# Attention values in one stationary tile: high and low parts side by side, their products added afterwards, and output blocks that hold both heads

## The chip, the cores and the metric

The kernel runs on one core of a Trainium2 chip. A core has TensorE (PE; its weight loads are shown as a queue of their own, PEld), VectorE (DVE), ScalarE (ACT), GpSimd (POOL) and SyncE (SP), which starts the transfers. Each works through its own instructions in order, and they wait for one another through semaphores. The metric is the time of one execution on the device in microseconds (us); lower is better.

## What is computed

The reference is a layer of two parts over 8 sequences of 512 rows and 256 columns. The first is a Mamba block (convolution, selective scan). The second, in which the change lies, is attention with mixtures of experts for values and outputs, then a feed-forward block. Cut to the part that matters:

```
D, H, P, E, K, F = (256, 16, 64, 8, 2, 1024)
def _moe_attn(x, Wq, Wk, Wv, Wo, Wsel_v, Wsel_o):
    q = _rope(jnp.einsum('bsd,hdp->bhsp', x, Wq))
    k = _rope(jnp.einsum('bsd,hdp->bhsp', x, Wk))
    gv = _gate(x, Wsel_v)
    v = jnp.einsum('bsd,bhse,hedp->bhsp', x, gv, Wv)
    att = jax.nn.softmax(jnp.einsum('bhsp,bhtp->bhst', q, k) / np.sqrt(P), axis=-1)
    o = jnp.einsum('bhst,bhtp->bhsp', att, v)
    go = _gate(x, Wsel_o)
    return jnp.einsum('bhsp,bhse,hepd->bsd', o, go, Wo)
```

There are 16 heads of 64 columns. `_gate` keeps the two largest of 8 expert scores in each row. An output of a head is multiplied by the gates of its 8 experts, which gives 8 x 64 rows for the contraction with `Wo`.

## The kernel before

The program has three stages. `stage_a` is the Mamba block, `stage_c` the feed-forward block. `stage_b` is the attention: the outer loop runs over 8 pairs of heads, the inner one over the 8 sequences, so there are 64 **batches** (one pair of heads, one sequence), with the same instructions in each. The last batch of a pair (`more_pairs`) also prepares the weights of the next pair; 7 of the 64 do so, and I call the end of such a batch a pair boundary.

Products are made of two parts: a float32 operand is split into a high part (a copy rounded by the type) and a low part (the operand minus the high part), and high*high, high*low and low*high are added in PSUM. ACT makes the high parts, DVE or POOL the low ones. `product` issues the three matmuls.

In a batch, TensorE runs in this order (function `batch` under `block.tensor`): `values` (expert values) mixed with `scores`; 16 transposes of 128x128 for the first head's probabilities (`turn_probabilities`); `attend(it, 0, c)` for 4 chunks c of the rows; 16 transposes for the second head and 4 of the gates (`turn_gates`); `attend(it, 1, c)`; then `spread_gates` 0 to 3 (they spread the output gates over the partitions, two blocks each) among the two `project_raw` (query and key of the next batch); then `project(it, j, n)` for 8 output blocks n.

`attend` multiplies the values, held still in the array, by the turned probabilities. The values of a head have 64 columns. Before, they lie twice side by side in each of two tiles (`vv[0]` high, `vv[1]` low, 128 columns each), so the output has the head's 64 rows twice, and one block of 128 rows is one head with two experts: blocks 0 to 3 are of the first head and need only `oT[:, 0]`, blocks 4 to 7 of the second. ACT copies these outputs out of PSUM (`keep_outputs`), DVE multiplies two blocks at a time by the spread gates (`gate_outputs` p = 0 to 3), ACT takes the high part (`high_outputs`), and the low part is POOL's for blocks 0 to 3 and DVE's for blocks 4 to 7 (`low_outputs`). `project(n)` waits for the low part of block n.

What else matters on the other engines: DVE does the rope of the next batch (`turn_raw`: two multiplications and a shuffle in place; `rotate`: their sum, into `qk_full`, which before shares its memory with `oT`), then `low_qk`; `tops` and POOL's `rank_one` to `rank_four` alternate to find the two largest gates of the next batch, ending in `gates`, which the next `gate_values` needs; `low_half` on POOL makes the low parts of `wv` and `wo` for the next pair. DVE's order in the tail is set by the order of calls in its `batch`:

```
                gate_outputs(it, 2)
                gate_outputs(it, 3)
                if more or more_pairs:
                    turn_raw(it + 1)
                    rotate(it + 1)
                low_outputs(it, 0)
                low_outputs(it, 1)
                if more or more_pairs:
                    tops(*coming, 2)
                low_outputs(it, 2)
                low_outputs(it, 3)
```

## Time and profile before

| what | value |
|---|---|
| three runs | 4522.73, 4522.21 and 4515.9 us, median 4522.21 |
| the profiled execution | 4524.23 us in all, its span 4522.4 us |
| PE (matmuls) | busy 3882.3 us, 86% of the span |
| PEld (weight loads) | busy 2704.3 us, 60% |
| DVE | busy 3556.1 us, 79% |
| POOL | busy 2873.1 us, 64% |
| ACT | busy 2045.4 us, 45% |
| granted TensorE clock | 0.911 of full speed over the span, 0.99 to 1.00 in the attention |

Stage B takes from about 1476 us (the first low part of `wv`) to about 4200 us of the span. Busy time of PE says little by itself: the records of successive matmuls overlap (each lasts 0.39 us while they start 0.23 us apart), so what PE's work costs is read from the starts, and what it waits for from the idle time in brackets.

### The profile page before, as it was taken

What the parts mean: (1) busy time and instruction counts of PE and PEld (TensorE: products, weight loads), DVE (VectorE), ACT (ScalarE), POOL (GpSimd) and SP (SyncE); (2) the same over time, 40 slices, a digit from 0 to 9 for tenths busy, and PEclk for the clock granted to TensorE, in tenths of its full rate; (3) what the DMA queues carried; (4) which work ended last, traced back from release to release, by engine and by line L of the source; (5) the groups of instructions that cost most, each with busy time, mean ns of one, the idle gap of its engine ahead of it and who ended that gap; (6) DMA issues with size and microseconds to landing.
All of it is one profiled execution on the core that took longest, in us unless ns stands there. A gap on an engine that the chain in (4) does not pass through costs nothing. (4 is left out here: it accounts for less than half of the span.)

```text
span 4522.4 us, 54798 instructions
## 1 busy us (share of the span) xinstructions
PE 3882.3 (86%) x16256; PEld 2704.3 (60%) x16256; DVE 3556.1 (79%) x3884; ACT 2045.4 (45%) x3761; POOL 2873.1 (64%) x2524
## 2 busy tenths in 40 slices
PE   6777776777764899999999999999999999999887
PEld 2233333333322677777777777777777777777676
DVE  5999999999995677677777677677677677677598
ACT  4544544545532344444444444444444444444443
POOL 2757757758663666666666766766666666666444
PEclk8887777877876999999999999999999999999898
DMA  1000000000002100000000000000100100000001
GB/s 37 0 10 14 24 9 14 24 10 14 19 10 95 45 14 14 35 14 14 35 10 18 35 9 19 35 9 9 39 14 9 39 14 9 19 14 12 31 28 42
DMA packets 48727, 97.83 MB, mean 22 GB/s; under 512 B 3571, under 2 KB 33139, under 8 KB 46229
## 3 DMA queue, kind: packets, MB, share of 16 engines
q1 hardware_dynamic: 47620, 92.94, 5.9%
q0 software_dynamic: 1040, 4.19, 0.2%
q8 instruction: 19, 0.31, 0.0%
q14 instruction: 48, 0.39, 0.0%
HBM read 80.34 MB, written 16.78 MB: 21 GB/s over the span
## 5 line engine op out<-in xcount | busy, mean ns | idle before, releaser
L702 DVE TENSOR_TENSOR_SCAN state<-dA,dBx 128x2048 f32<-128x2048 f32 x128 | 726.5, 5676 | 26.3 <-POOL y_part L289 21.3
L1230 ACT ACTIVATE prob<-ps_b,negmax 128x512 f32<-128x512 f32 x512 | 346.7, 688 | 849.6 <-DVE negmax L1345 849.6
L286 POOL TENSOR_TENSOR state<-state,c_copy 128x1024 f32<-128x1024 f32 x120 | 345.8, 2881 | 374.7 <-DVE state L702 374.7
L1339 DVE TENSOR_TENSOR vg<-ps_b,gates 128x1024 f32<-128x1024 f32 x256 | 313.6, 1225 | 307.0 <-PE ps_b L1072 307.0
L961 POOL TENSOR_TENSOR qk_full<-vg 128x512 f32<-128x512 f32 x256 | 329.9, 1289 | 329.4 <-DVE vg L1339 329.4
L1070 PE MATMUL ps_b<-ogT_high,wo_high 128*128 128x512 f32 x1024 | 413.6, 404 | 77.2 <-DVE ogT_low L1384 76.9
L549 ACT ACTIVATE dA<-dt,a_neg 128x511 f32<-128x511 f32 x512 | 327.8, 714 | 320.9 <-DVE state L702 320.6
L1070 PE MATMUL ps_b<-wv_high,xT_high 128*128 128x512 f32 x1024 | 419.9, 410 | 35.6 <-POOL wv_low L954 35.6
L372 PE MATMUL ps_a<-xp_high,ident_r 33*128 33x512 f32 x256 | 162.0, 633 | 331.5 <-DVE dBx L692 306.4
L289 POOL TENSOR_TENSOR y_part<-y_part,state 128x1024 f32<-128x1024 f32 x120 | 403.5, 3362 | 9.4
L1071 PE MATMUL ps_b<-wv_low,xT_high 128*128 128x512 f32 x1024 | 405.0, 395 | 0.0
L1072 PE MATMUL ps_b<-ogT_high,wo_low 128*128 128x512 f32 x1024 | 404.9, 395 | 0.0
L1072 PE MATMUL ps_b<-wv_high,xT_low 128*128 128x512 f32 x1024 | 403.1, 394 | 0.0
L1071 PE MATMUL ps_b<-ogT_low,wo_high 128*128 128x512 f32 x1024 | 402.6, 393 | 0.0
L1360 DVE TENSOR_TENSOR probT_low<-ps_b,probT_high 128x512 fp32r<-128x512 f32 x512 | 317.4, 683 | 90.3 <-ACT probT_high L1242 90.3
L975 POOL TENSOR_TENSOR ogT_low<-prob,ogT_high 128x512 fp32r<-128x512 f32 x256 | 324.0, 1296 | 91.6 <-ACT ogT_high L1261 91.6
L393 PE MATMUL ps_a<-state,ident 128*128 128x512 f32 x512 | 347.4, 816 | 24.8 <-DVE work L719 22.6
L372 PEld LDWEIGHTS ps_a<-xp_high,ident_r 33*128 33x128 f32 x256 | 58.8, 230 | 492.4 <-DVE dBx L692 395.5
L1345 DVE TENSOR_REDUCE negmax<-ps_b 128x2 f32<-128x1024 f32 x256 | 301.1, 1218 | 64.2 <-PE ps_b L1103 64.1
L1261 ACT ACTIVATE ogT_high<-ps_b 128x512 fp32r<-128x512 f32 x256 | 153.7, 601 | 310.4 <-PE ps_b L1072 310.4
L692 DVE TENSOR_TENSOR dBx<-du,ps_a 128x2048 f32<-128x2048 f32 x128 | 289.1, 2258 | 1.8 <-PE ps_a L373 1.8
L1242 ACT ACTIVATE probT_high<-ps_b 128x512 fp32r<-128x512 f32 x512 | 265.1, 605 | 53.3 <-PE ps_b L1114 53.3
(236 smaller groups left out, 9798.0 us busy)
## 6 DMA issues: line engine op xcount, KB each, us to landing
xT<-xT_scratch SPq DMA_DIRECT2D x65, 512.0 KB, 3.3
wv<-in_wv SPq DMA_DIRECT2D x8, 1024.0 KB, 4.9
wo<-in_wo SPq DMA_DIRECT2D x8, 1024.0 KB, 7.0
x_in<-in_x SPq DMA_DIRECT2D x8, 512.0 KB, 4.6
x_a<-in_x SPq DMA_DIRECT2D x8, 512.0 KB, 5.3
x_scratch<-x_a SPq DMA_DIRECT2D x8, 512.0 KB, 2.9
xT_scratch<-x2T SPq DMA_DIRECT2D x8, 512.0 KB, 2.6
scores_scratch<-sg SPq DMA_DIRECT2D x8, 512.0 KB, 3.5
```

The source lines that it names most:

```text
L286: pool.tensor_tensor(state, state, c, ALU.mult).then_inc(hc_part_done, 1)
L289: pool.tensor_tensor(y[:, :, :], y[:, :, :], state, ALU.add).then_inc(y_part_done, 1)
L393: mm = pe.matmul(ps[:, m, :], ident[:, :], h[n % 2][:, m, :], start=(n == 0), stop=(n == NS - 1))
L549: act.activation(dA[n % 2][:, m, 1:S], dt[par][:, m, 1:S], ACT.Exp, scale=a_neg[:, m, n:n + 1]).then_inc(dA_done, 1)
L702: dve.tensor_tensor_scan(h[n % 2][:, :, :].rearrange("p c s -> p (c s)"), dA[n % 2][:, :, :].rearrange("p c s -> p (c s)"), dBx[n % 2][:, ...
L961: pool.tensor_tensor(v4[:, at, :, :], vg[:, at, 0:4, :], vg[:, at, 4:8, :], ALU.add).then_inc(vsum_done, 1)
L975: pool.tensor_tensor(ogT[1][:, e, :], og[:, e, :], ogT[0][:, e, :].bitcast(F32), ALU.subtract).then_inc(oT_low0, 1)
L1070: pe.matmul(out, left(0), right(0), start=start, stop=False)
L1071: pe.matmul(out, left(0), right(1), start=False, stop=False)
L1072: return pe.matmul(out, left(1), right(0), start=False, stop=stop)
L1230: act.activation(prob[h][:, t, :], ps[:, score_bank(t) + h, :], ACT.Exp, bias=negmax[:, t, h:h + 1], accum_out=total[:, h, t:t + 1]).then_ ...
L1360: dve.tensor_tensor(probT[1][:, n % RING, :], ps[:, n % TT, :], probT[0][:, n % RING, :].bitcast(F32), ALU.subtract).then_inc(pT_low, 1)
```

## The change

Six things change, all in `stage_b` and in the layout of its weights.

1. The values lie in one tile `vv`, high part in columns 0 to 63 and low part in columns 64 to 127. `attend` issues two matmuls for a chunk instead of three: all 128 columns against the high probabilities, which gives high*high in output rows 0 to 63 and low*high in rows 64 to 127; and the 64 high columns against the low probabilities, into rows 0 to 63. For the last chunk the narrow one comes first.
2. The two halves of the output are added: ACT moves one half out of PSUM across the partitions (`move_part`, in place of `keep_outputs`), DVE adds the other (`add_parts`, new). The first head's sum goes to rows 0 to 63 of `oT`, the second's to rows 64 to 127.
3. An output block now holds one expert of both heads, so every `gate_outputs` needs both heads' sums. `wo` and `spread` are laid out to match.
4. `spread_gates(it, 0)` comes after the last `attend` instead of before it.
5. `oT` has its own memory; `rotate` waits no more for `gate_outputs`. DVE's `low_outputs(0)` and `(1)` come before and after the shuffle, `rotate` after them and `tops` 2.
6. At a pair boundary POOL makes the low parts of the next `wv` before `rank_three` and `rank_four`, and DVE does `tops` 2 after the last `low_outputs`.

The diff, cut to its core:

```
-        oT = qk_full
+        oT, aside = sb("oT", [P, S]), sb("aside", [P, S])
-        vv = parts("vv", [P, 2, TT, 2 * HP])
+        vv = sb("vv", [P, 2, TT, 2 * HP], F32R)
...
# block.gpsimd
             def low_values(it, h):
                 pool.wait_ge(v_high, it * 2 + h + 1)
-                pool.tensor_tensor(vv[1][:, h, :, :].rearrange("p t (c n) -> p t c n", c=2), v[:, h, :, :].unsqueeze(2).to_broadcast([P, TT, 2, HP]),
-                                   vv[0][:, h, :, :].bitcast(F32).rearrange("p t (c n) -> p t c n", c=2), ALU.subtract).then_inc(v_low, 1)
+                pool.tensor_tensor(vv[:, h, :, HP:2 * HP], v[:, h, :, :], vv[:, h, :, 0:HP].bitcast(F32), ALU.subtract).then_inc(v_low, 1)
...
                 if coming:
                     rank_two(it + 1, ahead)
-                    rank_three(it + 1)
-                    rank_four(it + 1, ahead)
                 if more_pairs:
                     low_half(j + 1, "wv", 0)
                     low_half(j + 1, "wv", 1)
+                if coming:
+                    rank_three(it + 1)
+                    rank_four(it + 1, ahead)
...
# block.tensor
-                product(ps[:, ATTEND_BANK[h], :], lambda u: vv[u][:, h, c, :], lambda u: probT[u][:, n % RING, :],
-                        c == 0, c == TT - 1).then_inc(pv_psum, 1)
+                bank, last = ATTEND_BANK[h], c == TT - 1
+                if last:
+                    pe.matmul(ps[0:HP, bank, :], vv[:, h, c, 0:HP], probT[1][:, n % RING, :], start=False, stop=False)
+                mm = pe.matmul(ps[:, bank, :], vv[:, h, c, :], probT[0][:, n % RING, :], start=(c == 0), stop=last)
+                if not last:
+                    mm = pe.matmul(ps[0:HP, bank, :], vv[:, h, c, 0:HP], probT[1][:, n % RING, :], start=False, stop=False)
+                mm.then_inc(pv_psum, 1)
...
-                for c in range(TT - 1):
+                for c in range(TT):
                     attend(it, 1, c)
                 spread_gates(it, 0)
-                attend(it, 1, TT - 1)
                 spread_gates(it, 1)
...
# block.scalar
-            def keep_outputs(it, h):
+            def move_part(it, h):
+
                 act.wait_ge(pv_psum, it * N + h * TT + TT)
-                act.activation(oT[:, h, :], ps[:, ATTEND_BANK[h], :], ACT.Copy).then_inc(oT_done, 1)
+                act.wait_ge(oT_done, it * 2 + h)
+                here, other = slice(h * HP, (h + 1) * HP), slice((1 - h) * HP, (2 - h) * HP)
+                act.activation(aside[here, :], ps[other, ATTEND_BANK[h], :], ACT.Copy).then_inc(part_moved, 1)
...
                 high_values(it, 1)
+                move_part(it, 0)
                 for n in range(TT, N):
                     high_probabilities(it, n)
                 high_gates(it)
-                keep_outputs(it, 0)
-                keep_outputs(it, 1)
+                move_part(it, 1)
...
# block.vector
+            def add_parts(it, h):
+
+                here = slice(h * HP, (h + 1) * HP)
+                dve.wait_ge(part_moved, it * 2 + h + 1)
+                dve.wait_ge(og_done, CREDIT + it * EP)
+                dve.tensor_tensor(oT[here, :], ps[here, ATTEND_BANK[h], :], aside[here, :], ALU.add).then_inc(oT_done, 1)
+
             def gate_outputs(it, p):
...
-                if e == 0:
-                    dve.wait_ge(oT_done, it * 2 + h + 1)
+                if p == 0:
+                    dve.wait_ge(oT_done, it * 2 + 2)
...
                     tops(*coming, 0)
+                add_parts(it, 0)
                 for n in range(TT, N):
                     low_probabilities(it, n)
                 low_gates(it)
+                add_parts(it, 1)
                 gate_outputs(it, 0)
...
                     turn_raw(it + 1)
+                low_outputs(it, 0)
+                if more or more_pairs:
+                    swap_halves(it + 1)
+                low_outputs(it, 1)
+                if more:
+                    tops(*coming, 2)
+                if more or more_pairs:
                     rotate(it + 1)
-                low_outputs(it, 0)
-                low_outputs(it, 1)
-                if more or more_pairs:
-                    tops(*coming, 2)
                 low_outputs(it, 2)
                 low_outputs(it, 3)
-                if more or more_pairs:
+                if more_pairs:
+                    tops(*coming, 2)
+                    low_qk(it + 1)
+                    tops(*coming, 3)
+                elif more:
                     tops(*coming, 3)
                     low_qk(it + 1)
```

The last two chunks of the second head on TensorE, before (the two last `attend` with `spread_gates` 0 between them and 1 behind; in such a row the moving operand stands first, then the stationary one, then the size of the output):

```order
L1071 MATMUL ps_b<-probT_low,vv_high 128x512
L1072 MATMUL ps_b<-probT_high,vv_low 128x512
L1142 MATMUL ps_b<-gT,spread 128x512 x2
L1129 REGISTER_ALU
L1070 MATMUL ps_b<-probT_high,vv_high 128x512
L1071 MATMUL ps_b<-probT_low,vv_high 128x512
L1072 MATMUL ps_b<-probT_high,vv_low 128x512
L1142 MATMUL ps_b<-gT,spread 128x512 x2
```

and after the change, the whole `attend` of the second head:

```order
L1133 MATMUL ps_b<-probT_high,vv 128x512
L1135 MATMUL ps_b<-probT_low,vv 64x512
L1129 REGISTER_ALU
L1133 MATMUL ps_b<-probT_high,vv 128x512
L1135 MATMUL ps_b<-probT_low,vv 64x512
L1129 REGISTER_ALU
L1133 MATMUL ps_b<-probT_high,vv 128x512
L1135 MATMUL ps_b<-probT_low,vv 64x512
L1129 REGISTER_ALU
L1132 MATMUL ps_b<-probT_low,vv 64x512
L1133 MATMUL ps_b<-probT_high,vv 128x512
L1147 MATMUL ps_b<-gT,spread 128x512 x4
```

Eight matmuls stand where twelve stood, wide and narrow ones in turn, and the four of the gates follow together.

DVE's tail of a batch (`turn_raw`, shuffle, `rotate`, `low_outputs`, the maxima of the ranking), before:

```order
L1317 TENSOR_TENSOR prob1<-ps_b,cos 128x1024
L1319 STREAM_SHUFFLE prob1<-prob1 128x1024
L1323 ISA
L1324 ISA
L1325 REGISTER_ALU
L1326 TENSOR_TENSOR qk_full<-prob1 128x1024
L1384 TENSOR_TENSOR ogT_low<-ps_b,ogT_high 128x512 x2
L1390 REGISTER_ALU
L1391 TENSOR_REDUCE top<-left 128x16
L1384 TENSOR_TENSOR ogT_low<-ps_b,ogT_high 128x512 x2
```

and after the change:

```order
L1323 TENSOR_TENSOR prob<-ps_b,cos 128x1024
L1399 TENSOR_TENSOR ogT_low<-ps_b,ogT_high 128x512
L1328 STREAM_SHUFFLE prob<-prob 128x1024
L1399 TENSOR_TENSOR ogT_low<-ps_b,ogT_high 128x512
L1405 REGISTER_ALU
L1406 TENSOR_REDUCE top<-left 128x16
L1332 ISA
L1333 REGISTER_ALU
L1334 TENSOR_TENSOR qk_full<-prob 128x1024
L1399 TENSOR_TENSOR ogT_low<-ps_b,ogT_high 128x512 x2
```

The first low part, which `project(4)` waits for, stood behind the shuffle and the sum and now stands ahead of both.

## Rows read from the trace of the kernel before

**Rows 1.** Waits of PE over stage B: us in total, times, longest

```profile
PE ps_b L1070 <- DVE ogT_low L1384: 76.9, 63, 1.3
PE ps_b L1070 <- POOL wv_low L954: 35.6, 7, 5.1
```

**Rows 2.** Busy time by engine in one batch, granted clock behind it

```profile
2609.12:2651.37 42.25, 40.78 (x202) 31.96 (x200) 31.09 (x39) 19.00 (x39) 27.27 (x33) 1.00 0.03 12
```

**Rows 3.** Timeline of PE in that batch: start us, duration, instruction [idle before <-releaser]

```profile
2625.80 0.50 PE L1070 MATMUL ps_b<-probT_high,vv_high 128*128 128x512 f32 x1 [0.24 <-DVE probT_low L1360]
...
2628.70 1.91 PE L1114 MATMUL ps_b<-ident,prob 128*128 128x128 f32 x16
...
2630.83 0.49 PE L1070 MATMUL ps_b<-probT_high,vv_high 128*128 128x512 f32 x1
...
2634.96 0.40 PE L1070 MATMUL ps_b<-xT_high,wqk_high 128*128 128x512 f32 x1
...
2638.68 0.40 PE L1070 MATMUL ps_b<-ogT_high,wo_high 128*128 128x512 f32 x1
...
2645.66 0.51 PE L1070 MATMUL ps_b<-ogT_high,wo_high 128*128 128x512 f32 x1 [1.21 <-DVE ogT_low L1384]
```

**Rows 4.** Timeline of DVE in the tail of that batch

```profile
2629.97 2.48 DVE L1360 TENSOR_TENSOR probT_low<-ps_b,probT_high 128x512 fp32r<-128x512 f32 x4 [1.41 <-ACT probT_high L1242]
...
2634.07 2.35 DVE L1377 TENSOR_TENSOR prob<-qk_full,ps_b 128x1024 f32<-128x1024 f32 x2 [0.90 <-PE ps_b L1142]
...
2640.01 1.22 DVE L1315 TENSOR_TENSOR prob<-ps_b,sin 128x1024 f32<-128x1024 f32 x1
...
2642.42 1.33 DVE L1319 STREAM_SHUFFLE prob<-prob 128x1024 f32<-128x1024 f32 x1
...
2644.92 1.28 DVE L1384 TENSOR_TENSOR ogT_low<-ps_b,ogT_high 128x512 fp32r<-128x512 f32 x2
...
2648.49 1.22 DVE L1330 TENSOR_TENSOR qk_low<-qk_full,qk_high 128x1024 fp32r<-128x1024 f32 x1
```

**Rows 5.** Timeline of PE: from `values` (128 rows used) to `scores` (64 rows used)

```profile
2611.64 0.39 PE L1072 MATMUL ps_b<-wv_high,xT_low 128*128 128x512 f32 x1
2611.96 0.50 PE L1103 MATMUL ps_b<-qk_high 64*128 64x512 f32 x2
2612.29 0.40 PE L1103 MATMUL ps_b<-qk_low,qk_high 64*128 64x512 f32 x2
```

**Rows 6.** Timeline of PE in stage A: `project_xp` holds 33 columns (128*33)

```profile
328.00 0.39 PE L373 MATMUL ps_a<-xp_low,ident_r 33*128 33x512 f32 x1
328.32 3.62 PE L357 MATMUL ps_a<-xc,w_xp 128*33 128x512 f32 x8
331.87 1.98 PE L393 MATMUL ps_a<-state,ident 128*128 128x512 f32 x4
```

**Rows 7.** Timeline of the weight loads there

```profile
328.78 0.11 PEld L357 LDWEIGHTS ps_a<-xc,w_xp 128*33 128x33 f32 x1 [0.32 <-issue]
329.20 0.11 PEld L357 LDWEIGHTS ps_a<-xc,w_xp 128*33 128x33 f32 x1 [0.32 <-issue]
...
332.41 0.19 PEld L393 LDWEIGHTS ps_a<-state,ident 128*128 128x128 f32 x1 [0.24 <-issue]
```

**Rows 8.** Timeline of ACT in the batch: the second `keep_outputs`

```profile
2634.69 0.60 ACT L1250 ACTIVATE qk_full<-ps_b 128x512 f32<-128x512 f32 x1 [2.30 <-PE ps_b L1072]
```

**Rows 9.** Timeline of POOL in the batch: low outputs, two steps of the ranking

```profile
2636.12 5.06 POOL L975 TENSOR_TENSOR ogT_low<-prob,ogT_high 128x512 fp32r<-128x512 f32 x4 [1.41 <-ACT ogT_high L1261]
...
2643.26 0.46 POOL L1007 TENSOR_TENSOR left<-hit,scores 128x128 f32<-128x128 f32 x1 [0.19 <-POOL hit L1004]
...
2648.65 1.32 POOL L991 TENSOR_TENSOR far<-rank,top_first 128x128 f32<-128x128 f32 x1 [0.40 <-DVE top_first L1391]
```

**Rows 10.** Timeline of PE at a pair boundary: the first `values` of the next pair

```profile
2867.95 0.80 PE L1070 MATMUL ps_b<-wv_high,xT_high 128*128 128x512 f32 x1 [5.10 <-POOL wv_low L954]
```

**Rows 11.** Timeline of POOL at that boundary

```profile
2863.23 4.66 POOL L954 TENSOR_TENSOR wv_low<-wv,wv_high 128x1024 fp32r<-128x1024 f32 x2
```

## What I predict, and why

> **What bounds the kernel now.** I read PE's waits first, then how busy the engines are in one batch, then that batch in order of time. In stage B, PE has two waits worth naming: 1.2 us in each of 63 batches for DVE's low part of block 4, and 5.1 us at each of 7 pair boundaries for POOL's low part of `wv` [rows 1]. Otherwise TensorE is what everything else waits for: a batch takes 42.25 us and PE's records cover 40.78 of it, at the full clock of 2.4 GHz (granted 1.00); DVE is busy for 31.1, POOL for 27.3, ACT for 19.0 [rows 2]. The change moves the time if it shortens PE's issue or takes these waits away. Times below are the trace's less 2600.
>
> The batch on PE [rows 3]: `attend` 0 starts at 25.80 and its 12 matmuls end at 28.70 (2.90; so 0.233 each and 0.10 for the first). 20 transposes take 2.13, to 30.83. `attend` 1 and the first four `spread_gates` matmuls end at 34.96. From there to the first `project` is 3.72 (38.68). Four blocks of `project` should follow in 4 x 1.40 = 5.6, but block 4 starts only at 45.66, after a stall of 1.21. What it waits for is on DVE [rows 4]: `gate_outputs` starts at 34.07, the rope at 40.01, and the low part comes only behind the shuffle (42.42) and the sum, at 44.92. The next batch begins at 51.37.
>
> **Term 1, the matmuls saved and the switches bought.** A batch loses 8 of 24 `attend` matmuls: 8 x 0.233 = 1.87 us. But the array now goes back and forth between 128 and 64 columns. Nothing in `attend` shows that price; two places bound it. Going from full to half rows, PE starts the next matmul 0.32 after the last (0.09 more than 0.233), and the second 0.33 after that (0.10 more) [rows 5]. With columns it is alike: 0.32 into the 33-column matmuls [rows 6], then 0.46 to the second of them (328.78, where a load goes out with the matmul ahead of it) and 0.42 to 0.43 from then on (329.20), so 0.03 more for the first load; on the way out, the eighth and the first full one are 3.55 - 0.46 - 6 x 0.43 = 0.51 apart (0.08 to 0.09 more), and the second full one follows after 0.54 (332.41; 0.11 more) [rows 6, 7]. So a switch costs a break of 0.09 plus the first weight load, which no longer hides: 0.03 for 33 columns, 0.10 to 0.11 for 128, about 0.05 for 64. In: 0.14; out: 0.19. A head has three of each (the swapped last chunk saves a pair): 1.0 us, against 4 x 0.233 = 0.93 saved. **Each `attend` becomes 0.07 us longer, not 0.93 shorter.** Bounds for the mean switch: nothing (0) to 0.26 (if the next matmul starts only when the record of the last, 0.39, has ended: 0.16, plus 0.10).
>
> The Trainium skill rules against this change: "TensorEngine Tiling (Array Packing)", Key Properties, has it that a change of tiling mode drains the engine. The trace agrees that something is lost at each one, the 0.09 us above; were the drain the whole rest of a record (0.16), the 12 switches would cost 3.1 us in place of 2.0, which is a rival below. For the load of 64 columns, which no row here has, "TensorE: Matmul & The Clock Gate", LDWEIGHTS, gives an estimate of 53 ns (columns / 1.2 GHz); by it the 12 switches would come to the same 2.0 us.
>
> **Term 2, the walk through a batch.**
> - `attend` 0 ends at 28.70 + 0.07 = 28.77, the transposes at 30.90.
> - New on DVE ahead of the second head's low probabilities: `add_parts` 0. The last matmul's record ends at about 28.9, ACT's copy of 64x512 takes 0.60 as its copy of 128x512 does [rows 8] (I take rows to be free; bounds 0.6 and 1.2), DVE starts at about 29.7 and takes one place of 2.48 / 4 = 0.60 [rows 4]. The low probabilities start at 30.3, not 29.97; with 0.68 for the first one, `attend` 1 starts at 31.05 (before 30.83).
> - `attend` 1 takes 0.10 + 8 x 0.233 + 1.0 = 2.96: 34.00. The four matmuls of the gates, 0.94: 34.95. Before: 34.96. PE is thus where it was, ready for `project` at 38.67.
> - The two heads' sum comes later. The last `attend` matmul ends at 34.17, ACT's copy 34.2 to 34.83, `add_parts` 1 (0.69) to 35.57, so `gate_outputs` starts at 35.6: 1.54 later. From its start to POOL's first low output took 2.05 (36.12), then 5.06 / 4 = 1.27 for one [rows 4, 9]: block 0 is ready at about 38.95. **PE waits 0.34 us in a new place**, before block 0, and starts at 39.0. POOL's next ones (40.2, 41.5, 42.7) stay ahead of the blocks (40.5, 41.9, 43.3).
> - Block 4 is due at 39.0 + 0.1 + 5.6 = 44.7. DVE no longer waits for PE between its `gate_outputs`: four at 1.15 and `tops` 1 (0.2) bring the rope to 40.4, its two multiplications (2.41) to 42.8, and the low part stands at 43.45. **The stall of 1.21 is gone.** Shuffle 1.33, low part 1 at 45.4 (due 46.1); `tops` 2 (POOL's `left` ended 2.6 us after its low outputs, at 43.72 [rows 9]; now 42.7 + 2.6 = 45.3), `rotate` 1.2, low part 2 at 47.4 (due 47.5: it just holds), low part 3 at 48.0 (due 48.9).
> - The batch ends at 39.1 + 8 x 1.40 = 50.3 instead of 51.37: **1.06 us less**. `low_qk` ends at about 50.1, `gates` at about 52.3; they are needed when the two first `values` are done, 2.84 after the batch's start (53.1) [rows 2, 5]. A step on POOL that runs beside a DVE sum of two SBUF tiles is held up (1.32 beside `low_qk`, where `left`, of the same size, took 0.46) [rows 4, 9]; this is counted.
> - Covered and costing nothing: POOL's and ACT's value parts at half size (they end 0.5 us sooner each; PE's wait is for the probabilities), the new layout of `wo`, `oT` in its own memory.
>
> 63 batches x 1.06 = 67 us.
>
> **Term 3, the pair boundary.** Before, PE is ready at about 2862.7, POOL starts on `wv` only at 2863.23, PE goes on at 2867.95, and its next matmuls run at half clock (1.2 GHz; the first record is 0.80 instead of 0.50): some seven at 0.21 more, 1.5 us by my estimate [rows 10, 11]. With the stall of 5.3, 6.8 in all. After, POOL starts on `wv` at 45.3, 5 us before PE is ready. The two halves take 4.66 [rows 11], plus up to 2.4 for `rotate` and `low_qk`, which hold POOL up: 50.0 to 52.4, PE being ready at 50.3. I take the latter, a stall of 2.1. Then the ranking ends about 4.5 us after the pair's start instead of ahead of the values, and POOL's low parts of `wo` (as long as those of `wv`) hold up its value sums to 9.3; ACT's `high_values` 0 then keeps back the last exponentials, and the transposes come 1.1 to 1.5 us late. Left: 3.7 of 6.8. 7 x 3.1 = 21 us (5.2 x 7 = 36 if POOL is not held up; 7 x 1.5 = 10 if the clock falls all the same).
>
> **The sum.** 67 + 21 = 88. The profiled execution took 4524.23, of which the span is 4522.4, and lies 2.0 above the median 4522.21. 4522.2 - 88 = 4434.
>
> **The rivals.**
> - *Switches are as good as free* between wide and narrow matmuls of one accumulation. Then `attend` 0 goes at the pace of DVE's low probabilities (0.60 a chunk) and ends at 28.1, the low probabilities of head 1 start at 29.6, `attend` 1 ends at 32.6, `gate_outputs` starts at 34.2, `project` at 37.6, and the batch ends at 48.9: 2.5 less. 63 x 2.5 + 7 x 3 to 5 = 180 to 190: 4335. The 33-column matmuls speak against it [rows 6]; for it only that no narrow matmul here follows a wide one of the same bank. 13%.
> - *Switches wait for the whole record* (0.26 each): 12 x 0.26 = 3.1 instead of 2.0, all of it on the path: the batch ends at 51.4, as before. Only the boundary is left: 4500. 11%.
> - *Slower: a switch overlaps nothing*, neither the record of the last matmul (0.16) nor the whole record of the load (0.19): 0.35. 12 x 0.35 = 4.2, 2.2 more than counted; 1.1 more per batch than before. 4522 + 69 - 21 = 4570. It decides from 0.28 a switch: there 12 x 0.28 = 3.4 eats 1.06 and the boundary's 0.33 a batch. Both kinds of switch in the trace speak against it [rows 5 to 7]. 9%.
> - *The copy across partitions costs double* (1.2 instead of 0.6): it stands before the low probabilities of head 1 and before `gate_outputs`, 0.6 each. The batch gains nothing: about 4500. 7%.
> - *The boundary keeps its stall*, because the low parts are held up further or the clock falls: 4455. Inside my range.
>
> **How the numbers follow.** Forecast and its neighbours (4400 to 4475) 60%, at 4434. The time grows one for one with switches, copy and `add_parts`, so half a switch's error (0.04 x 12 = 0.5 us a batch) is 30 us: the range goes from 4375, half way to the free switches, to 4495. A measurement of this kernel tells 0.2% (9 us). Faster 0.87, within 0.2% 0.04, slower 0.09.
>
> **What would show it.** Right: starts in `attend` 0.37 to 0.42 apart at each change of width; no idle time of PE before block 4 but 0.3 before block 0, now for POOL's low output; `gate_outputs` 1.5 later against the batch's start; a batch of 41.2; PE's waits for `wv` at 7 boundaries about 2. Wrong: starts 0.23 apart throughout (the first rival), or a batch of 42 or more with `attend` over 3.3 us a head. What I can least see is whether a narrow and a wide matmul into the same bank follow one another as those of stage A do [rows 6], which go to different banks.

## The result, and the profile after the change

| | before | after |
|---|---|---|
| median | 4521.15 us (4 runs, 4515.9 to 4522.73) | 4359.82 us (4 runs, 4355.63 to 4360.78) |
| profiled execution, span | 4524.23, 4522.4 | 4360.78, 4358.8 |
| granted TensorE clock over the span | 0.911 | 0.909 |

The ratio is 0.9643, with a 95% interval of 0.9627 to 0.966: 161 us less, where I had forecast 88 and a range that ended 15 us above the result. The direction was right, the size and one of the reasons were not.

One batch after the change, from the first matmul of `values` to that of the next batch (length, then busy time with the number of instructions for PE, PEld, DVE, ACT, POOL, then the granted clock); it answers to [rows 2]:

```profile
2619.73:2659.70 39.97, 39.69 (x194) 29.56 (x192) 31.89 (x41) 18.79 (x39) 26.92 (x34) 1.00 0.04 13
```

39.97 instead of 42.25 us: 2.28 less, eight matmuls fewer (a few records are missing on each side), two instructions more on DVE, at the same clock. The additions to the output, one a batch, are 39.97 us apart in an ordinary batch and 43.00 where a pair ends (before 42.25 and 49.22, means of seven). After the change the batch behind such a boundary is longer too, 40.44; before, it was 42.26, as any other. From the first to the last of these 64 it took 4239.5 - 1532.0 = 2707.5 us before and 4074.6 - 1530.2 = 2544.4 after: the 163 us less in the span are all there, in stage B.

PE's waits, which answer to [rows 1] (total, times, longest):

```profile
PE ps_b L1133 <- DVE probT_low L1368: 21.5, 64, 1.1
PE ps_b L1070 <- DVE ogT_low L1399: 10.8, 7, 1.5
```

The wait before block 4 is gone from the ordinary batches, and that for `wv` at the seven boundaries is gone altogether. Seven waits of 1.5 us for DVE's low output parts stand there instead.

The same batch in order of time on PE, to be held against [rows 3]:

```profile
2636.42 0.50 PE L1133 MATMUL ps_b<-probT_high,vv 128*128 128x512 f32 x1 [0.24 <-DVE probT_low L1368]
2636.76 0.39 PE L1135 MATMUL ps_b<-probT_low,vv 128*64 128x512 f32 x1
2637.02 0.50 PE L1133 MATMUL ps_b<-probT_high,vv 128*128 128x512 f32 x1
2637.36 0.39 PE L1135 MATMUL ps_b<-probT_low,vv 128*64 128x512 f32 x1
...
2638.21 0.44 PE L1132 MATMUL ps_b<-probT_low,vv 128*64 128x512 f32 x1
2638.49 0.39 PE L1133 MATMUL ps_b<-probT_high,vv 128*128 128x512 f32 x1
2638.73 1.91 PE L1114 MATMUL ps_b<-ident,prob 128*128 128x128 f32 x16
...
2641.07 0.50 PE L1133 MATMUL ps_b<-probT_high,vv 128*128 128x512 f32 x1
...
2644.62 0.39 PE L1070 MATMUL ps_b<-xT_high,wqk_high 128*128 128x512 f32 x1
...
2648.42 0.47 PE L1070 MATMUL ps_b<-ogT_high,wo_high 128*128 128x512 f32 x1
```

A chunk (wide, then narrow) starts 0.60 us after the one before it, and that is the pace of DVE's low probabilities: four in 2.48. Where nothing is waited for, from the last narrow matmul to the wide one and to the transposes, 0.28 and 0.24 pass. The price that I had put there was 0.42 for the way out. The batch in its parts, from these starts:

| part of the batch | before | predicted | after |
|---|---|---|---|
| `attend` 0 | 2.90 | 2.97 | 2.31 |
| 20 transposes | 2.13 | 2.28 | 2.34 |
| `attend` 1, first four of the gates | 4.13 | 3.90 | 3.55 |
| first `project_raw` to block 0 | 3.72 | 4.05 | 3.80 |
| block 0 to the next batch | 12.69 | 11.3 | 11.28 |

The last line, the stall, came out as forecast. The others came out 1.2 us shorter than predicted, taken together.

DVE in that batch, against [rows 4]:

```profile
2639.73 0.68 DVE L1383 TENSOR_TENSOR oT<-ps_b,aside 64x512 f32<-64x512 f32 x1 [0.79 <-ACT aside L1256]
2640.34 2.47 DVE L1368 TENSOR_TENSOR probT_low<-ps_b,probT_high 128x512 fp32r<-128x512 f32 x4
...
2645.01 2.35 DVE L1392 TENSOR_TENSOR prob<-oT,ps_b 128x1024 f32<-128x1024 f32 x2
...
2652.13 0.68 DVE L1399 TENSOR_TENSOR ogT_low<-ps_b,ogT_high 128x512 fp32r<-128x512 f32 x1
...
2652.73 1.37 DVE L1328 STREAM_SHUFFLE prob<-prob 128x1024 f32<-128x1024 f32 x1
2653.95 0.71 DVE L1399 TENSOR_TENSOR ogT_low<-ps_b,ogT_high 128x512 fp32r<-128x512 f32 x1
```

`add_parts` of 64x512 takes 0.68 and ACT's copy 0.60, as assumed. `gate_outputs` comes 0.39 after `project_raw` starts, before the change 0.89 ahead of it. Block 4's low part starts at 52.13 and is there in time.

### The profile page after: what moved, and what is told of

It is laid out like the page before. It is cut to its first block and busy times, and to the rows that moved or that the text cites. A ratio compares the mean times of both kernels' runs of the same rounds, so it can differ in the third digit from the quotient of the medians.

```text
span 4358.8 us, 54031 instructions
## 1 busy us (share of the span) xinstructions
PE 3803.9 (87%) x15744; PEld 2541.1 (58%) x15744; DVE 3630.8 (83%) x4012; ACT 2029.6 (47%) x3761; POOL 2849.6 (65%) x2524
## 5 line engine op out<-in xcount | busy, mean ns | idle before, releaser
L393 PE MATMUL ps_a<-state,ident 128*128 128x512 f32 x512 | 345.9, 813 | 24.8 <-DVE work L719 22.7
```

The costliest lines, as they stand in the source:

```text
L393: mm = pe.matmul(ps[:, m, :], ident[:, :], h[n % 2][:, m, :], start=(n == 0), stop=(n == NS - 1))
```

## The experiments

Every kernel starts from the changed one unless it says otherwise. Each expectation names its theories anew. The runs come in three questions: what a change of width costs, which part of the change brings what, and what is left to gain.

### What a change of width costs

**e1: all four low probabilities are waited for first; the first head keeps 128 and 64 columns in turn, the second has 128 throughout.**

```
-                pe.wait_ge(pT_low, it * N + n + 1)
+                if c == 0:
+                    pe.wait_ge(pT_low, it * N + n + TT)
...
+                cols = HP if h == 0 else P
```

> The changed kernel, with each head's attend held back until all four low probabilities are there, so that nothing in it waits; head 0 alternates 128 and 64 columns as changed, head 1 uses 128 columns in both matmuls (it adds low*low too). Theory A (the price of my prediction: 0.14 us into 64 columns, 0.19 out): starts in head 0 are 0.28 to 0.42 apart, the eight take 2.96 us to the next instruction, head 1's take 1.96. Theory B (changing the width is free): 0.233 apart in both, both take 1.96 us. Under either the kernel is slower than the changed one, by 1.4 to 3 us a batch (4450 to 4550), since the waiting is taken on purpose.

4590.64 us, one run. The first head's starts were 0.33, 0.24 and 0.23 apart, then 0.33 to 0.43, but the later ones at half clock: the granted clock was 1.00 from 2649.87 to 2650.67 and 0.50 from 2651.00 to 2652.70, after PE had stood idle for 2.03 us. The second head, all wide, at 1.00: 0.35, then 0.22 to 0.24 throughout. So in this batch three starts alone spoke for a free change of width; too few.

**e14: the same with the heads exchanged, so that the alternation has the full clock.**

```
-                cols = HP if h == 0 else P
+                cols = HP if h == 1 else P
```

> As e1, with the heads exchanged: the second head, which ran at full clock in e1, has 128 and 64 columns in turn, the first head 128 columns throughout; attend waits for all four low probabilities first. Theory D (a change of width costs nothing with the rounded type): the 8 matmuls of the second head start 0.23 apart, the whole 1.85 to 1.95 us, as the wide ones of e1 did. The prediction's price (0.14 into narrow, 0.19 out): 0.37 to 0.42 apart, 2.8 to 2.9 us. Time in either case about 4590 us, as in e1, or up to 60 more by the prediction's price.

4567.8 us, one run. Timeline of PE, second head, granted clock 1.00 over these rows:

```profile
2601.73 0.51 PE L1135 MATMUL ps_b<-probT_high,vv 128*128 128x512 f32 x1 [1.79 <-DVE probT_low L1370]
2602.07 0.40 PE L1137 MATMUL ps_b<-probT_low,vv 128*64 128x512 f32 x1
2602.30 0.40 PE L1135 MATMUL ps_b<-probT_high,vv 128*128 128x512 f32 x1
2602.54 0.39 PE L1137 MATMUL ps_b<-probT_low,vv 128*64 128x512 f32 x1
2602.77 0.40 PE L1135 MATMUL ps_b<-probT_high,vv 128*128 128x512 f32 x1
...
2603.47 0.40 PE L1135 MATMUL ps_b<-probT_high,vv 128*128 128x512 f32 x1
2603.71 1.10 PE L1149 MATMUL ps_b<-gT,spread 128*128 128x512 f32 x4
```

After the first start (0.34) every matmul follows 0.23 or 0.24 after the last, wide to narrow, narrow to wide and narrow to narrow. Eight take 1.98 us. The other batches of this trace agree: without the first start of each head, and at a granted clock of 1.00, 126 narrow matmuls follow a wide one and 189 wide ones a narrow one after 0.227 to 0.238 us, and in the other head 247 wide ones follow one another after 0.225 to 0.238. The change of width costs nothing.

**e4: 128 columns in both matmuls, so that no width changes.**

```
-  pe.matmul(ps[0:HP, bank, :], vv[:, h, c, 0:HP], probT[1][:, n % RING, :], ...)
+  pe.matmul(ps[:, bank, :], vv[:, h, c, :], probT[1][:, n % RING, :], ...)
```

> The changed kernel with 128 columns in both matmuls of a chunk, so that the width never changes (it adds low*low too). Theory A (each change costs 0.14 to 0.19): 12 changes fewer, but DVE's pace of 0.60 us a chunk then bounds attend; it gains wherever the changes, not the pace, held it: up to 0.5 us a batch, 4330. Theory B (free): same time, 4360 within 9 us.

4360.22 us (4358.98 to 4364.71), ratio to before 0.9644 (0.9628 to 0.966): the same as the changed kernel. An ordinary batch is not shorter without the changes of width but 0.10 us longer (40.07 against 39.97). By itself this would not settle it, since DVE's 0.60 a chunk would cover a small price; with e14 it does.

**e2: what was different in stage A? 33 columns in the first head, and float32 instead of the rounded type in the second.**

```
+                cols = XP if h == 0 else HP
+                as_is = (lambda v: v) if h == 0 else (lambda v: v.bitcast(F32))
```

> The same with all ready, to find what makes stage A's 33-column matmuls break off. Head 0: the narrow matmul has 33 columns (the other 31 are left out of high*low). Head 1: both matmuls read their operands as float32 instead of the rounded type, 128 and 64 columns in turn. Theory C (a width that is no full 32 or 64 makes the break): head 0 breaks, about 0.3 to 0.4 between starts, head 1 does not (0.43 between records). Theory D (float32 matmuls, issued as two records each, make it): head 0 runs at 0.233, head 1 has 0.09 to 0.2 more at every change of width. Theory E (neither; it lies in what stands before and behind in stage A, such as the bank): 0.233 in head 0 and 0.43 in head 1 throughout.

4951.86 us, one run (float32 matmuls come as two records each). With 33 columns there was no break: in the batch looked at 0.34, 0.23, and 0.43 once the clock was 0.50; over all batches 89 starts from wide to narrow and 128 from narrow to wide, at a granted clock of 1.00, lie 0.225 to 0.240 apart. With float32 there was one, at a granted clock of 1.00:

```profile
2655.52 1.12 PE L1136 MATMUL ps_b<-probT_high,vv 128*128 128x512 f32 x2
2656.57 1.07 PE L1138 MATMUL ps_b<-probT_low,vv 128*64 128x512 f32 x2
2657.57 1.12 PE L1136 MATMUL ps_b<-probT_high,vv 128*128 128x512 f32 x2
2658.63 1.07 PE L1138 MATMUL ps_b<-probT_low,vv 128*64 128x512 f32 x2
2659.54 1.02 PE L1135 MATMUL ps_b<-probT_low,vv 128*64 128x512 f32 x2
```

A wide and a narrow matmul take 2.05 us together (2655.52 to 2657.57), where their four records would take 1.72 at the 0.43 of [rows 6, 7]: 0.33 more for one change each way. Read record by record, it is the prediction's price to the hundredth: 0.52 from a wide matmul's last record to a narrow one's first and the same on the way back (0.09 more than 0.43), then 0.53 to a wide matmul's second record (0.10 more) and 0.48 to a narrow one's (0.05 more), in each of 192 such places. That is 0.14 in and 0.19 out. The 0.91 from narrow to narrow still holds the 0.05 of the change before it. So it is the type, not the number of columns, that separates stage A from `attend`: the price was right for float32, and there is none with the rounded type.

**e3: `w_xp` of stage A filled up to 128 columns with zeros, the attention as it is.**

```
-        w_xp = sb("w_xp", [P, CB, XP])
+        w_xp = sb("w_xp", [P, CB, 128])
```

> The changed kernel, with the 33 columns of w_xp in stage A padded by zeros to 128, so that project_xp has the width of sum_y behind it. If the width made the 0.51 and 0.54 us behind project_xp (0.09 and 0.11 over 0.43), the step shrinks to 0.43 and the four records of sum_y take 1.88 instead of 1.98 us. If they stay, what I read as the price of a change of width was something else. The time stays within 5 us of the changed kernel's 4360 in either case.

4355.66 us, one run. The place of [rows 6], from the last four of `project_xp` to the next ones:

```profile
327.06 1.88 PE L357 MATMUL ps_a<-xc,w_xp 128*128 128x512 f32 x4
328.78 1.88 PE L393 MATMUL ps_a<-state,ident 128*128 128x512 f32 x4
```

Four starts in 1.72, that is 0.43 each, and no break of 0.08 to 0.11 on the way out: the four matmuls of L393 have 1.88 instead of 1.98. There the width did make the break that I had read. The way in is another matter:

```profile
324.93 0.39 PE L373 MATMUL ps_a<-xp_low,ident_r 33*128 33x512 f32 x1
325.24 3.70 PE L357 MATMUL ps_a<-xc,w_xp 128*128 128x512 f32 x8
```

It took 0.32 in [rows 6] and takes 0.31 here, with 128 columns on both sides. So the width did not make it. The matmul ahead of it uses 33 rows (33*128), and rows and type change there together. I had read the way out rightly and carried it to matmuls of another type; the way in I had read as a change of columns, which it is not.

**e13: the other source, [rows 5]. The scores contract over all 128 rows instead of one head's 64 (they are then the sum of both heads').**

```
-                        rows = slice(h * HP, (h + 1) * HP)
+                        rows = slice(0, P)
```

> The changed kernel, in which the 24 matmuls of the scores in a batch contract over all 128 rows instead of the 64 of one head (the scores are then the sum of both heads'). In the kernel before, going from 128 to 64 rows cost 0.09 and then 0.10 us, and as much on the way back, in matmuls of the rounded type. Theory E (the change of rows makes that break): the breaks are gone, every matmul starts 0.23 after the last, 24 of them take 5.5 us instead of the 12 pairs' 2.8 plus 4 x 0.19 at each way in and out. Theory F (the break has to do with the operands or banks of the scores, not with rows): 0.32 and 0.33 us stay at the way in. Time by either: 2 to 2.8 us more per batch, 4490 to 4540 us.

4458.29 us, one run, less than either theory gave: an ordinary batch took 41.79 us, 1.8 more than the 39.97 of the changed kernel, where 2 to 2.8 had been expected. On PE:

```profile
2706.20 0.39 PE L1072 MATMUL ps_b<-wv_high,xT_low 128*128 128x512 f32 x1
2706.42 0.62 PE L1103 MATMUL ps_b<-qk_high 128*128 128x512 f32 x2
2706.88 0.61 PE L1103 MATMUL ps_b<-qk_low,qk_high 128*128 128x512 f32 x2
...
2709.14 0.39 PE L1070 MATMUL ps_b<-wv_high,xT_high 128*128 128x512 f32 x1
```

0.22 into the scores, 0.46 for each two, and 0.23 on the way out, where 0.32 and 0.33 had stood. So going from 128 rows to 64 and back does break the sequence in the rounded type, and a change of columns does not. e13 takes away two things at once, the change of rows and the starting together of two matmuls on 64 rows each; it does not tell which of them makes the break. It also shows what the half rows give: the two heads' matmuls of a pair start together, 0.23 a pair, against 0.46 here.

### Which part brings what

**e5: the order in DVE's tail put back** (shuffle and `rotate` before `low_outputs` 0 and 1; `oT` keeps its own memory).

```
-                low_outputs(it, 0)
                 if more or more_pairs:
                     swap_halves(it + 1)
+                    rotate(it + 1)
+                low_outputs(it, 0)
                 low_outputs(it, 1)
...
-                if more or more_pairs:
-                    rotate(it + 1)
```

> The changed kernel, in which only the order on VectorE in the tail of a batch is put back: shuffle and rotate before the first two low output parts (the outputs keep their own memory). By theory A (what the two matmuls of a chunk save reaches the end only because the low part of block 4 no longer stands behind the rope) that part is ready at 2612.16 + 1.33 + 1.22 + 0.64 = 2615.35 where it is due at 2614.16: 1.2 us a batch come back, 63 x 1.2 = 75, so about 4435 us, with a wait of PE before block 4 in every batch. By theory B (the tail is no longer what PE waits for, the gain of the attention products stands alone) it stays within 10 us of 4360.

4433.13 us (4431.85 to 4433.98), ratio 0.9802 (0.9785 to 0.9818). PE's waits:

```profile
PE ps_b L1070 <- DVE ogT_low L1399: 72.6, 63, 1.2
```

73 us slower than the changed kernel, and 72.6 us of new waits in 63 batches, where theory A had 75.

**e6: the order at the boundary put back**

```
                 if coming:
                     rank_two(it + 1, ahead)
+                if coming:
+                    rank_three(it + 1)
+                    rank_four(it + 1, ahead)
                 if more_pairs:
                     low_half(j + 1, "wv", 0)
                     low_half(j + 1, "wv", 1)
-                if coming:
-                    rank_three(it + 1)
-                    rank_four(it + 1, ahead)
```

(with DVE's two maxima as before).

> The changed kernel, in which only the order at the pair boundary is put back (the ranking before the low parts of the next wv on GpSimd; maxima of the ranking as before on VectorE). By theory A (the boundary's gain comes from this order) the boundary's batch goes from 42.99 us back to about 39.97 + 6.8 = 46.8: 7 x 3.8 = 27 us, so about 4387 us, with waits of PE for wv_low of about 5 us at 7 places. By theory B (the gain is a matter of GpSimd being free earlier in every batch, whatever the order) under 10 us: 4365 to 4370, with waits for wv_low of about 1 us.

4384.58 us (4382.79 to 4386.57), ratio 0.9694 (0.9678 to 0.9711): 25 us. The wait is back, 42.1 us in seven places, longer than before the change, since PE is ready earlier and POOL is not:

```profile
PE ps_b L1070 <- POOL wv_low L954: 42.1, 7, 6.0
```

**e7: the kernel before with the new tail of DVE alone.**

```
-        oT = qk_full
+        oT = sb("oT", [P, 2, S])
...
                     turn_raw(it + 1)
-                    rotate(it + 1)
                 low_outputs(it, 0)
+                if more or more_pairs:
+                    swap_halves(it + 1)
                 low_outputs(it, 1)
                 if more or more_pairs:
                     tops(*coming, 2)
+                    rotate(it + 1)
```

> The kernel before, with nothing but the outputs in a memory of their own and VectorE's new order in the tail of a batch (low parts of blocks 4 and 5 among the rope). By theory A this takes away PE's wait of 1.21 us before block 4 in 63 batches: 76 us, so about 4445 us, and the rest of the gain (4445 to 4360) is that of the products and the boundary. By theory B (the wait only moves, to block 6 or to the next batch's scores, which now come later) less than 25 us: above 4495.

4440.14 us (4430.6 to 4440.67), ratio 0.9812 (0.9795 to 0.9828): 81 us. No wait for `ogT_low` is left, and that for `wv_low` grew from 35.6 to 42.6 us.

**e8: the kernel before with the new order at the boundary alone** (the reverse of e6's diff).

> The kernel before, with nothing but the new order at the pair boundary. The prediction's sum for the boundary (7 x 3.1 = 21 us) gives 4500 us. By theory A (VectorE's rotate is held up as much as GpSimd is, and TensorE keeps its clock) the boundary goes from 49.1 to 42.25 + 3.0: 7 x 3.8 = 27, so 4494 us. By theory B (the gain at the boundary needs the other parts of the change too) 0 to 10 us: 4511 or more.

4499.58 us (4495.24 to 4501.71), ratio 0.9946 (0.993 to 0.9963): 22 us. Nothing is left of the waits for `wv`, but DVE's low part is waited for as often as before and up to 3.2 us long, 13.8 us more in all than in [rows 1]:

```profile
PE ps_b L1071 <- DVE ogT_low L1385: 90.7, 63, 3.2
```

**e9: both orders put back; what remains are the two matmuls a chunk, the added halves and the common blocks.** Its diff is those of e5 and e6.

> The changed kernel with both orders put back, VectorE's tail as in e5 and the pair boundary as in e6: what is left of the change is the two matmuls of a chunk, the half results added, and the blocks of both heads. By the prediction's term for these (12 changes of width at 0.17 make each attend 0.07 us longer, and PE waits before block 0) there is nothing to gain: 4521 or more. By theory A (no price for a change of width; the batch gains 1.0 us from the products, and the three gains add up) 4360 + 73 + 25 = 4458 us.

4470.24 us (4468.61 to 4471.24), ratio 0.9883 (0.9866 to 0.9899): 52 us, or 0.8 a batch, 12 us less than theory A had expected. Its two waits are those of [rows 1], 72.5 and 35.6 us, so the 52 us lie in TensorE's way from `attend` 0 to the first `project`: an ordinary batch is 0.87 shorter (41.38 against 42.25), and the first four lines of the table above give 12.88 against 12.00. The three parts taken alone make 52 + 81 + 22 = 155 of 161.

### What is left

**e10: the first head's part moved and added later**

```
                 high_values(it, 1)
-                move_part(it, 0)
...
                 high_gates(it)
+                move_part(it, 0)
                 move_part(it, 1)
...
                 low_gates(it)
+                add_parts(it, 0)
                 add_parts(it, 1)
```

(the first is ACT's order, the second DVE's; `move_part` of the second head no longer waits for `add_parts` of the first, which now comes behind it).

> The changed kernel, in which ACT moves the first head's part after the high gates and VectorE adds it after the low gates, no longer ahead of the second head's probabilities. By theory A (TensorE's first matmul of the second head waits for VectorE's low probabilities, which stand behind this addition of 0.6 us) attend of the second head starts 0.45 us sooner and the batch shrinks by as much: 63 x 0.45 = 28 us, about 4332. By theory B (the outputs for the gates come later by the same addition, which then stands before them, and PE waits before block 0 or block 4 instead) 4355 to 4375.

**e11: and `rotate` later at the boundaries.**

```
-                if more or more_pairs:
+                if more:
                     rotate(it + 1)
                 low_outputs(it, 2)
                 low_outputs(it, 3)
                 if more_pairs:
+                    rotate(it + 1)
```

> As e10, and at the 7 pair boundaries VectorE's rotate comes after the last two low output parts, so that it does not stand, held up by GpSimd, before the part that block 6 waits for. By theory A this takes 1.5 us at 7 places: 10 us less than e10. By theory B (GpSimd is then held up by something else, or the scores of the next batch come late) within 5 us of e10.

**e12: the changed kernel again, on the same chip.**

> The changed kernel as it is, beside the three others on the same chip: 4360 us, ratio to before 0.9644.

e12: 4353.56 us (4349.4 to 4361.53), ratio 0.9628 (0.9612 to 0.9644). e10: 4335.42 (4333.49 to 4337.75), ratio 0.9587 (0.9571 to 0.9603), 18 us less; its span is 20.0 less (4332.3 against 4352.3). I had expected 28. On PE in e10:

```profile
2629.65 0.60 PE L1121 MATMUL ps_b<-ident,out_gate 128*128 128x128 f32 x4
2630.01 0.48 PE L1133 MATMUL ps_b<-probT_high,vv 128*128 128x512 f32 x1
2630.32 0.40 PE L1135 MATMUL ps_b<-probT_low,vv 128*64 128x512 f32 x1
```

`attend` 1 follows the gates' transposes after 0.36 instead of 0.60, so the wait for DVE was 0.24 us there and not the whole 0.45. An ordinary batch is 39.71 us instead of 39.97, which makes 15 us; the batches behind a boundary, 39.69 instead of 40.44, bring 5 more.

At the boundary e10 did something that I had not meant. DVE and POOL there:

```profile
2762.52 1.21 DVE L1334 TENSOR_TENSOR qk_full<-prob 128x1024 f32<-128x1024 f32 x1
```

```profile
2762.53 6.79 POOL L954 TENSOR_TENSOR wv_low<-wv,wv_high 128x1024 fp32r<-128x1024 f32 x2
```

`rotate` starts 0.01 us ahead of `low_half` and takes its usual 1.21, and POOL takes 6.79; in the changed kernel `rotate` starts 0.09 behind and takes 3.40, and POOL takes 5.74. So in six of seven boundaries PE waits for `wv` instead of block 6:

```profile
PE ps_b L1070 <- POOL wv_low L954: 8.8, 6, 1.5
```

e11: 4336.19 (4334.91 to 4337.59), the same as e10. It therefore had no wait of 1.5 before block 6 left to take away. The wait for `wv` shrinks to 3.0 us in 8 places, and PE waits for ACT's exponentials in the next batch instead:

```profile
PE ps_b L1103 <- ACT prob L1234: 6.8, 14, 0.6
```

That is theory B, within 5 us of e10: the scores of the next batch come late, and what is left of the waiting stands elsewhere.

## Why the prediction was wrong where it was

**The step that failed is the price of a switch in term 1**, "0.14 in, 0.19 out", 12 of them a batch. e14 measured 0 to 0.01 each. The prediction's rows were real, but none of them was of what `attend` does, which keeps its rows and has the rounded type. [rows 5] are of a change of rows (e13 removes their break). The way in of [rows 6] is one too, from 33 rows to 128, and I had taken it for a change of columns; it stays when the columns are alike (e3). The way out of [rows 6, 7] is a change of columns (e3 removes it), but of float32 matmuls, and for those the whole price is right (e2 finds 0.14 in and 0.19 out in `attend`). I had named a gap at the end ("what I can least see"), but it was the bank and not the type; the free switch had 13%. The Trainium skill states in "TensorEngine Tiling (Array Packing)", Key Properties, that a change of tiling mode drains the engine. Between 128 and 64 rows something is lost, 0.09 and then 0.10 us, which is gone in e13; between 128 and 64 columns of the rounded type e14 shows no loss, and no run here shows whether that change counts as one of mode.

**What stands in its place.** The walk with free switches is the prediction's first rival: `attend` at DVE's 0.60 a chunk, a batch less by 2.5. Measured: 0.60 a chunk and 2.28. It gave 4335, 25 us too low, because it took the batch 0.2 too short (14 us) and up to 5 us a boundary where 3.4 were won back; the transposes took 2.34 and `attend` 1 still waited 0.24 for the low probabilities behind `add_parts` 0 (e10).

**Term 2, the tail.** Right. The stall of 1.21 is gone: e5 brings back 73 us, e7 alone gives 81, against 63 x 1.21 = 76. The predicted wait of 0.34 before block 0 did not come. `gate_outputs` starts 25.28 us into the batch, before 24.95: 0.33 later and not 1.54, because both `attend` were shorter. The net of 1.06 us a batch was therefore 1.2 too small, which is about 76 us and all of what lies between 4434 and 4360.

**Term 3, the boundary.** Its size was nearly right, its form was not. Predicted 3.1 of 6.8 us won back. Measured: a boundary costs 6.9 us more than an ordinary batch before; after, it costs 43.00 - 39.97 = 3.03, and 40.44 - 39.97 = 0.47 more in the batch behind it. So 3.5 are left (3.7 predicted) and 3.4 are won back: 24 us, against 22 in e8, 25 in e6 and the 21 forecast. But PE has no wait for `wv`. DVE and POOL at a boundary of the changed kernel, and PE's block 6:

```profile
2774.43 3.40 DVE L1334 TENSOR_TENSOR qk_full<-prob 128x1024 f32<-128x1024 f32 x1
2777.75 1.28 DVE L1399 TENSOR_TENSOR ogT_low<-ps_b,ogT_high 128x512 fp32r<-128x512 f32 x2
...
2779.15 2.01 DVE L1338 TENSOR_TENSOR qk_low<-qk_full,qk_high 128x1024 fp32r<-128x1024 f32 x1
```

```profile
2774.34 5.74 POOL L954 TENSOR_TENSOR wv_low<-wv,wv_high 128x1024 fp32r<-128x1024 f32 x2
```

```profile
2778.49 0.50 PE L1070 MATMUL ps_b<-ogT_high,wo_high 128*128 128x512 f32 x1 [1.55 <-DVE ogT_low L1399]
```

I had counted only that DVE holds POOL up (up to 2.4; measured 5.74 - 4.66 = 1.08). The other direction is larger: `rotate` takes 3.40 instead of 1.22 beside POOL's `low_half`, so the low parts behind it are late and PE waits 1.55 before block 6. POOL itself is done with `wv` at 2780.08 and PE comes at 2781.39. The half clock after the stall did not come: granted 1.00 from 2781 to 2784. In the batch behind the boundary the late values that I had predicted do appear, 0.34 us before the transposes and then, in the second head, on PE and on DVE:

```profile
2804.44 0.50 PE L1133 MATMUL ps_b<-probT_high,vv 128*128 128x512 f32 x1 [1.10 <-DVE probT_low L1368]
```

```profile
2803.10 0.68 DVE L1383 TENSOR_TENSOR oT<-ps_b,aside 64x512 f32<-64x512 f32 x1 [1.44 <-ACT aside L1256]
```

ACT moves the first head's part behind the high parts of the second head's values, DVE adds it ahead of the low probabilities, and PE waits 1.10 where an ordinary batch has 0.24. e10, which puts both behind the second head's probabilities, has no such wait left.

**The sum.** Sixty-two batches at 2.27, seven boundaries at 3.4, less 1.6 for the last batch (41.27 us after, 39.65 before): 163 us, which is the difference of the spans. The last batch took 39.73 in e12; what makes it vary was not looked into.

**The chances.** Faster at 0.87 was right. The range of 4375 to 4495 ended 59 of the 99 us on the way to the free switches, not half way as I wrote; with a 13% case at 4335 and bounds for the unknown price that began at 0 it should have reached down to it.

## What to carry to other kernels

Before the price of an event is taken from another stage, compare everything that the row states: rows, columns and above all the type of the operands; two of the three being alike was not enough. Where a price can be zero, redo the walk with zero as the forecast's equal: it then shows what paces the stage instead, here DVE's 0.60 us a chunk, so that narrower matmuls bring nothing more (e4) and an earlier DVE does (e10, 18 us).

A long GpSimd operation on two tiles of SBUF should not be put beside a short VectorE one of the same kind that TensorE waits for. The boundary's order paid for itself all the same, by 22 us.

## What the hardware did that I had not expected

- A change of width from 128 to 64 or 33 columns costs nothing with operands of the rounded type (0.23 to 0.24 us from start to start; e14, e2). With float32 a change from 128 to 64 columns costs 0.14 us and one back 0.19 (e2).
- VectorE's sum and GpSimd's low part of two SBUF tiles hold each other up, and a hundredth of a microsecond goes with which of them pays: with the sum 0.09 us behind, it takes 3.40 instead of 1.22 and the two halves 5.74 instead of 4.66; with the sum 0.01 us ahead, 1.21 and 6.79 (e10). The times fit one operation at a time, in turn: POOL's first half ends at 2776.75, and the sum ends 1.08 later, at 2777.83; the second half takes 3.37 instead of 2.41. In e10 it is POOL's first half that takes 3.47, and its second, beside `low_qk`, 3.35. That the start decides is my reading of these two places; it was not varied by itself.
- After 2.03 us of idle time PE ran three intervals at full clock and fell to 0.50 only then (e1), and in the other head, after 1.30, not at all; in the batch shown of e14 it kept 1.00 after 1.79 and, in the first head, after 2.03 as well. What decides between these was not tried.
